# Order of two steps in the vector engine's turn: normalised rows and slots

## The chip, the cores and the metric

The kernel runs on one core of a Trainium2 chip. The metric is the device time of one execution in microseconds (us), the median of several runs. The engines are named as the profile names them: PE (matmul), PEld (its weight load), DVE (vector), ACT (scalar), POOL (GpSimd) and SP (its queue issues most DMAs).

## What is computed

There are 16 graphs of 512 nodes with 128 features. A graph attention layer comes first, then a layer with 16 experts of which each node uses two:

```python
x = x + gnn(layernorm(x), adj, ...)       # 16 graphs, softmax over masked scores, elu
x = x + ffn(layernorm(x), ...)            # top-2 of 16 experts, relu, layernorm with gamma, beta
```

In the second layer the gate's two best experts are found for each node, and the result is the weighted sum of these two experts alone.

## The kernel before

There are two stages. In the graph stage every engine runs a loop of turns over k, written out by hand, and each turn holds steps for several graphs at different depths: in turn k the attention scores are those of graph k, the output of the attention (`elu_parts`, `elu_sum`, L1109 to L1121) and its statistics (`stats`) are those of graph k-2, and the gate and the slots are those of graph k-3. In the expert stage the tokens, sorted by expert in bins in DRAM, are taken in tiles of 128.

Each engine has one in-order queue; what ties them together are semaphores. These steps are near the change:

- `mask(k + 1)` (L1074, DVE): adjacency of the next graph to a bf16 tile `no_edge`.
- `rows(k - 2)` (L1138, DVE): four instructions that make the normalised rows of graph k-2 from `x_sb`, with mean and rstd, into `row_out`. It waits for `s_rs2`, the rstd from POOL, and for the bins' scatters of graph k-6; its end is `s_x2n`.
- `slot(k - 3)` (L1274 to L1308, DVE): 15 small instructions, chained by waits on the engine's own results, that turn the ranks in PSUM `bank[7]` into row numbers of the bins, `slots`. It waits for `s_rank` from PE; its end is `s_slot`.
- POOL in turn k (L581, L567, L572): eight indirect DMAs that scatter the rows of graph k-4 into the bins, the first of which waits for `s_slot` and `s_row_out` of that graph, and between them two rstd computations of two instructions each (`var_eps`, then a pow): the one for the features of graph k+2 after the fourth scatter and the one for the rows of graph k-2 after the fifth (it waits for the `mv` of `stats(k - 2)`).
- PE in turn k: after the first two score blocks, `rows_transposes(k - 3)` (L911) into `bank[7]`, then the logits, later the ranks of the same graph.
- ACT in turn k: `rows_out(k - 3)` copies the rows for the second expert (L709), and `gate_weights(k - 3)` writes their weights.
- SP: the load of the next adjacency waits for `mask`.

The two waits of the PE step are these:

```python
            def rows_transposes(g):
                pe.wait_ge(s_x2n, g + 1)
                wait_for(pe, s_slot, g)
```

Of the kernel before, what the change touches and what calls it, by code (L numbers as in the profile page):

```python
# [19 lines left out]
def graph_attention_and_routed_experts(nc, x, adj, W, a_1, a_2, a_12, W_1, W_2, gate_w, gate_b, w1, b1, w2, b2,  # L20
                                       gamma, beta, out):
    G, N, D = x.shape
# [43 lines left out]
    with ExitStack() as ctx:  # L66
# [162 lines left out]
        def wait_for(eng, s, value):  # L229

            if not isinstance(value, int) or value > 0:
                eng.wait_ge(s, value)
# [39 lines left out]
        def has(k, back):  # L272

            return not isinstance(k, int) or 0 <= k - back < G
# [156 lines left out]
        def bin_wait(eng, g):  # L431

            if g >= 0:
                eng.wait_ge(s_bin[g % RB], 16 * K * TPG * (g // RB + 1))
# [629 lines left out]
        def _(dve):  # L1064
            V = nc.vector
            def xt(k, i):
                t = k * TPG + i
                return x_sb[:, t, :] if isinstance(t, int) else x_sb[:, bass.ds(t, 1), :].rearrange("p a d -> p (a d)")

            def mask(k):  # L1070

                dve.wait_ge(s_adj, 16 * (k + 1))
                wait_for(dve, s_s, k * TPG)
                V.tensor_scalar(no_edge[:, :, :], adj_sb[:, :, :], 0.0, NEG_INF, ALU.is_le, ALU.mult).then_inc(s_mask, 1)  # L1074
# [16 lines left out]
            def scores(k, i):  # L1091

                dve.wait_ge(s_relu, k * TPG + i + 1)
                wait_for(dve, s_pt, (k - 1) * TPG + i + 1)
                settle(dve)
                V.tensor_tensor_reduce(prob[:, i, :], bank[i % 2][:, :], relu4[:, i % 2, :], -ALPHA, 3e38,  # L1096
                                       ALU.add, ALU.min, row_min[:, i:i + 1]).then_inc(s_em, 1)

            def inverse_sums(g):

                dve.wait_ge(s_exp, (g + 1) * TPG)
                V.reciprocal(rinv[:, :], tiles_of(row_sum, g)).then_inc(s_rinv, 1)

            def elu_parts(g, b):

                dve.wait_ge(s_rinv, g + 1)
                dve.wait_ge(s_pv, (g + 1) * TPG)
                for i in range(TPG):
                    last = V.scalar_tensor_tensor(out=z[:, i, :], in0=bank[6][:, i * P:(i + 1) * P],  # L1109
                                                  scalar=rinv[:, i:i + 1], in1=vh[:, b, i, D:2 * D], op0=ALU.mult,  # L1110
                                                  op1=ALU.add)
                last.then_inc(s_z, 1)
            def elu_sum(g):

                zs = Steps(dve, s_zs, g, 2)
                dve.wait_ge(s_z, g + 1)
                zs.did(V.scalar_tensor_tensor(out=xg_of(g), in0=z[:, :, :], scalar=0.0, in1=xg_of(g),
                                              op0=ALU.max, op1=ALU.add))
                dve.wait_ge(s_e, g + 1)
                zs.wait()  # L1120
                zs.did(V.scalar_tensor_tensor(out=xg_of(g), in0=z_exp[:, :, :], scalar=1.0, in1=xg_of(g),  # L1121
                                              op0=ALU.min, op1=ALU.add))
                zs.wait()
                zs.end()

            def feature_shift(g):

                dve.wait_ge(s_rs1, g + 1)
                wait_for(dve, s_feat, g)
                V.scalar_tensor_tensor(out=feat_shift[:, :], in0=mv[:, 0:TPG, 0:1].rearrange("p a b -> p (a b)"), scalar=-1.0,  # L1130
                                       in1=rstd[:, 0:TPG], op0=ALU.mult, op1=ALU.mult).then_inc(s_fshift, 1)

            def rows(g):

                dve.wait_ge(s_rs2, g + 1)
                bin_wait(dve, g - RB)
                for i in range(TPG):
                    last = V.tensor_scalar(row_out[:, g % RB, 0, i, 0:D], xt(g, i), mv[:, TPG + i, 0:1],  # L1138
                                           rstd[:, TPG + i:TPG + i + 1], ALU.subtract, ALU.mult)
                last.then_inc(s_x2n, 1)  # L1140

            def query_weights():

                dve.wait_ge(s_wt_sb, 5)
                dve.wait_ge(s_wt, 3)
                V.tensor_reduce(M_rows[:, 0:1], bank[2][:, 0:D], AX_X, ALU.add).then_inc(s_M, 1)
                dve.wait_ge(s_M, 1)
                V.tensor_scalar(M_rows[:, 1:2], M_rows[:, 0:1], u2[:, 0:1], -1.0 / D, ALU.subtract, ALU.mult).then_inc(s_M, 1)
                dve.wait_ge(s_M, 2)
                V.tensor_scalar(M_sb[:, :], bank[2][:, 0:D], M_rows[:, 1:2], None, ALU.add).then_inc(s_M, 1)  # L1150

            def query_bias():

                dve.wait_ge(s_wt, 4)
                V.scalar_tensor_tensor(out=u1[:, :], in0=bank[1][:, 2 * D:2 * D + 1], scalar=-1.0 / D, in1=u1[:, :],
                                       op0=ALU.mult, op1=ALU.add).then_inc(s_u1, 1)
                V.scalar_tensor_tensor(out=W21[:, :], in0=bank[3][:, 0:2 * D], scalar=-1.0 / D, in1=W21[:, :],
                                       op0=ALU.mult, op1=ALU.add).then_inc(s_W21, 1)
                dve.wait_ge(s_wt, 5)
                dve.wait_ge(s_u1, 1)  # L1160
                V.tensor_tensor(u1[:, :], u1[:, :], bank[0][:, 0:1], ALU.subtract).then_inc(s_u1, 1)

            def first_stats(g):
                dve.wait_ge(s_x[g % 3], 16 * (g // 3 + 1))
                stats(g, 0, s_bn1, s_mv1)

            def bias_cut():

                c = Steps(dve, s_cut, 0, CUTS)
                dve.wait_ge(s_b2, 16)  # L1170
                c.did(V.tensor_copy(b2_part[:, 0, :], b2_rows[:, :]))
                c.wait()
                c.did(V.tensor_tensor(b2_rest[:, 0, :], b2_rows[:, :], b2_part[:, 0, :], ALU.subtract))
                c.wait()
                c.did(V.tensor_copy(b2_part[:, 1, :], b2_rest[:, 0, :]))
                c.wait()
                c.did(V.tensor_tensor(b2_rest[:, 1, :], b2_rest[:, 0, :], b2_part[:, 1, :], ALU.subtract))
                c.wait()
                c.did(V.tensor_copy(b2_part[:, 2, :], b2_rest[:, 1, :]))
                c.end()  # L1180

            def body(k, b, h):
                if k == -2:
                    first_stats(0)
                    query_weights()
                    feature_shift(0)
                    query_bias()
                    return
                if k == -1:
                    mask(0)  # L1190
                    first_stats(1)
                    return
                if k == SPLIT_AT:
                    bias_cut()
                if has(k, 0):
                    scores(k, 0)
                if has(k, 2):
                    elu_parts(k - 2, b)
                if has(k, 0):
                    scores(k, 1)  # L1200
                if k == 0:
                    feature_shift(1)
                if has(k, -2):
                    first_stats(k + 2)
                if k == GROUPS[0][1] + 3:
                    tile_table(0)
                if has(k, 3):
                    gate(k - 3)
                if has(k, 2):
                    elu_sum(k - 2)  # L1210
                    stats(k - 2, TPG, s_bn2, s_mv2)
                if has(k, 1):
                    inverse_sums(k - 1)
                if has(k, 0):
                    scores(k, 2)
                    scores(k, 3)
                if has(k, -2):
                    feature_shift(k + 2)
                if has(k, -1):
                    mask(k + 1)  # L1220
                if has(k, 3):
                    slot(k - 3)
                if has(k, 2) and k < G:
                    rows(k - 2)
                if k == G - 2:
                    dve.wait_ge(s_late, 16 * LATE)
                    dve.wait_ge(s_tab_done, 1)
                    experts.fetch(0)
                if k == G - 1:
                    for t in range(4):  # L1230
                        weights_copy(t)
                    dve.wait_ge(s_b1, 1)
                    V.tensor_copy(b1_cols[:, :], bank[5][:, 0:E * FC]).then_inc(s_b1_cols, 1)
# [301 lines left out]
```

## Time and profile before

| what | value |
| --- | --- |
| time, median of 3 runs | 571.02 us |
| lowest and highest run | 568.17 and 571.75 us |
| span of the profiled execution, first to last instruction | 499.1 us |
| a turn of the graph stage in the middle | 15.27 us |
| busy over the span | PE 85%, PEld 73%, DVE 78%, ACT 64%, POOL 65% |
| granted TensorE clock, mean | 0.953 |

The span leaves out what lies before the first and after the last instruction. Times in the trace count from the span's start. A row of a timeline can hold several equal instructions in a row (x4); its duration then runs from the first start to the last end, and the next instruction can start a little before that end.

### The profile page before, as it was taken

The page shows a single profiled execution, that of the slowest core. Times are in us where ns is not written, and L with a number is a line of the kernel's source. Part 1 is how long each engine was busy: PE and PEld are TensorE (multiplying, and loading weights), DVE is VectorE, ACT ScalarE, POOL GpSimd, SP SyncE. Part 2 cuts the span into 40 slices and gives each one's busy share as a digit, 9 for nine tenths or more (in the row PEclk, how much of TensorE's full clock was granted, in tenths as well). Part 3 has the DMA queues.
Part 4 walks back from the last instruction along what each step waited for, and adds up shares of the span by engine and source line. Part 5 has one row for each costly group of instructions (what it writes and reads, how often), then busy time and mean ns, then how long its engine had stood idle before and what let it go on. Part 6 is the DMA issues. An engine that isn't in the chain of part 4 may idle for free.

```text
span 499.1 us, 11531 instructions
## 1 busy us (share of the span) xinstructions
PE 426.5 (85%) x3175; PEld 364.5 (73%) x3197; DVE 390.3 (78%) x1800; ACT 317.1 (64%) x859; POOL 321.9 (65%) x336
## 2 busy tenths in 40 slices
PE   4869999999998999989989979999999999898000
PEld 3347777776776767767668979999999999798000
DVE  5224788989889898898887968668979997787564
ACT  3468888889877798787774657556665665553000
POOL 2121226776777777866566777788777777777772
PEclk9989999999999999999998999999999999999555
DMA  8632576875366652645611255666777776665522
GB/s 253 196 115 66 195 215 213 262 233 156 73 210 230 178 154 67 224 128 183 178 33 34 65 139 142 170 163 162 198 191 198 199 210 167 153 164 137 129 72 66
DMA packets 82275, 78.84 MB, mean 158 GB/s; under 512 B 7795, under 2 KB 67619, under 8 KB 80934
## 3 DMA queue, kind: packets, MB, share of 16 engines
q1 hardware_dynamic: 73446, 60.99, 42.4%
q0 software_dynamic: 8192, 16.86, 12.6%
q8 instruction: 28, 0.46, 0.4%
q10 hardware_dynamic: 576, 0.26, 0.2%
q14 instruction: 33, 0.27, 0.2%
HBM read 44.44 MB, written 33.65 MB: 156 GB/s over the span
## 4 chain that ended last, share of the span: by engine, by line
PE 47%; DVE 24%; ACT 11%; issue 8%; POOL 5%; DMA 3%; DVEq 1%; ACTq 0%; POOLq 0%; SPq 0%
PE bank L1019 12%; PE bank L1004 11%; POOL yy L634 5%; PE bank L902 4%; PE bank L880 3%; PE bank L862 3%; PE bank L872 3%; DVE no_edge L1074 3%; DVE row_out L1138 3%; DMA yy<-expert_results,slots 3%; PE bank L919 2%; PE bank L991 2%; ACT relu L671 2%; ACT prob L675 2%; PE bank L911 2%
## 5 line engine op out<-in xcount | busy, mean ns | idle before, releaser
L581 POOL DMA_INDIRECT expert_bins<-row_out,slots x128 | 140.2, 1095 | 45.5 <-issue 39.6
L634 POOL DMA_INDIRECT yy<-expert_results,slots x128 | 134.6, 1052 | 39.1 <-issue 33.3
L786 ACT ACTIVATE hidT<-bank,b_cols 128x128 f32<-128x128 f32 x316 | 86.4, 383 | 53.2 <-PE bank L1004 47.5
L1019 PE MATMUL bank<-w_sb,hidT 128*128 x632 | 93.8, 291 | 0.0
L1019 PEld LDWEIGHTS bank<-w_sb,hidT 128*128 128x128 f32 x632 | 84.2, 194 | 2.0
L1004 PE MATMUL bank<-xgT,w_cur 128*128 128x128 f32 x632 | 79.6, 280 | 0.1
L1004 PEld LDWEIGHTS bank<-xgT,w_cur 128*128 128x128 f32 x632 | 75.8, 196 | 0.2 <-issue 0.2
L880 PEld LDWEIGHTS bank<-vh,probT 128*128 128x128 f32 x512 | 63.3, 192 | 14.7 <-issue 13.9
L872 PE MATMUL bank<-featT,qT 128*128 128x512 f32 x128 | 68.2, 615 | 5.2 <-ACT qT L704 2.4
L1096 DVE CUSTOM_DVE_ANT_0 prob<-bank,relu 128x512 f32<-128x512 f32 x64 | 43.5, 682 | 32.9 <-ACT relu L671 29.7
L880 PE MATMUL bank<-vh,probT 128*128 128x128 f32 x512 | 65.5, 276 | 0.5 <-ACT probT L666 0.5
L567 POOL TENSOR_SCALAR var_eps<-mv 128x4 f32<-128x4 f32 x32 | 8.3, 259 | 78.3 <-DVE mv L1085 78.0
L1368 DVE SCALAR_TENSOR_TENSOR y<-bank,xg 128x128 f32<-128x128 f32 x158 | 47.2, 344 | 13.1 <-PE bank L1019 13.0
L675 ACT ACTIVATE prob<-prob,row_min 128x512 f32<-128x512 f32 x64 | 45.8, 716 | 14.6 <-DVE row_min L1096 14.6
L666 ACT COPY probT<-bank 128x512 f32<-128x512 f32 x64 | 37.1, 579 | 25.6 <-PE bank L880 24.7
L671 ACT ACTIVATE relu<-bank 128x512 f32<-128x512 f32 x64 | 37.5, 587 | 7.7 <-PE bank L872 7.7
L794 ACT ACTIVATE final_root<-final_var 128x4 f32<-128x4 f32 x16 | 3.5, 219 | 56.5 <-DVE final_var L1389 56.5
L1337 DVE COPY w_cur<-w_all 128x256 f32 x158 | 36.6, 293 | 3.3 <-issue 1.9
L572 POOL TENSOR_TENSOR rstd<-var_eps,half 128x4 f32<-128x4 f32 x32 | 35.8, 1119 | 5.1 <-ACT feat L716 2.6
L862 PEld LDWEIGHTS bank<-ident,prob 128*128 128x128 f32 x256 | 31.1, 147 | 10.2 <-issue 5.4
L1017 PE MATMUL bank<-b_sum,ones_bf 96*128 x158 | 35.3, 223 | 3.1 <-DVE y L1368 3.1
L862 PE MATMUL bank<-ident,prob 128*128 128x128 f32 x256 | 36.9, 278 | 0.9 <-ACT prob L675 0.9
(143 smaller groups left out, 750.1 us busy)
## 6 DMA issues: line engine op xcount, KB each, us to landing
adj_sb<-in_adj_dram SPq DMA_DIRECT2D x16, 1024.0 KB, 6.4
expert_bins<-xg SPq DMA_DIRECT2D x10, 1032.0 KB, 8.6
expert_results<-y SPq DMA_DIRECT2D x78, 128.0 KB
xg<-expert_bins SPq DMA_DIRECT2D x38, 258.0 KB, 4.1
x_sb<-in_x_dram SPq DMA_DIRECT2D x16, 256.0 KB, 8.5
out_dram<-x_sb SPq DMA_DIRECT2D x15, 256.0 KB
expert_bins<-row_out,slots POOLq DMA_INDIRECT x128, 3.4
w_all<-in_L_ffn_w_dram SPq DMA_DIRECT2D x1, 2048.0 KB, 14.4
```

The lines of the kernel that those rows point to most:

```text
L581: nc.gpsimd.indirect_dma_start(bins[u], bass.IndirectOffsetOnAxis(ap=slots[:, g, i, j:j + 1], axis=0), row_out[:, r, j, i, :], None).then_ ...
L634: nc.gpsimd.indirect_dma_start(yy[:, b, i, j * D:(j + 1) * D], None, results[0:rows, :], bass.IndirectOffsetOnAxis(ap=slots[:, g, i, j:j + 1],
L671: nc.scalar.activation(relu4[:, i % 2, :], bank[i % 2][:, :], ACT.Relu, scale=4.0).then_inc(s_relu, 1)
L675: nc.scalar.activation(prob[:, i, :], prob[:, i, :], ACT.Exp, bias=row_min[:, i:i + 1], scale=-1.0, accum_out=tile_at(row_sum, k, i)).then ...
L786: r = nc.scalar.activation(hidT[:, t % NB, c * P:(c + 1) * P], hidden_of(t, c), ACT.Relu, bias=b1_cols[:, bass.ds(e * FC + c, 1)])
L862: last = nc.tensor.transpose(bank[2 + i % 2][:, c * P:(c + 1) * P], prob[:, i, c * P:(c + 1) * P], ident[:, :])
L872: mm(bank[i % 2][:, :], qT[:, b, i * P:(i + 1) * P], featT[:, b, :], start=False, stop=True).then_inc(s_s, 1)
L880: last = mm(bank[6][:, i * P:(i + 1) * P], probT[:, i % 2, c * P:(c + 1) * P], vh[:, b, c, 0:D], start=(c == 0), stop=(c == TPG - 1))
L1004: m1 = mm(hidden_of(t, c), w1_cur[:, t % WS, c * P:(c + 1) * P], xgT[:, t % NB, :], start=True, stop=True)
L1019: m2 = mm(out_psum(t), hidT[:, t % NB, c * P:(c + 1) * P], w2_sb[:, bass.ds((e * FC + c) * D, D)], start=False, stop=(c == FC - 1))
L1096: V.tensor_tensor_reduce(prob[:, i, :], bank[i % 2][:, :], relu4[:, i % 2, :], -ALPHA, 3e38, ALU.add, ALU.min, row_min[:, i:i + 1]).then_i ...
L1368: V.scalar_tensor_tensor(out=y[:, y_slot(t), :], in0=out_psum(t), scalar=xg[:, v, D:D + 1], in1=xg[:, v, 0:D], op0=ALU.mult, op1=ALU.add). ...
```

## The change

In DVE's turn the rows of graph k-2 are made before the slots of graph k-3; before it was the other way round. Nothing else is changed.

```diff
                 if has(k, -1):
                     mask(k + 1)
+                if has(k, 2) and k < G:
+                    rows(k - 2)
                 if has(k, 3):
                     slot(k - 3)
-                if has(k, 2) and k < G:
-                    rows(k - 2)
                 if k == G - 2:
                     dve.wait_ge(s_late, 16 * LATE)
                     dve.wait_ge(s_tab_done, 1)
```

## Rows read from the trace of the kernel before

**Rows 1.** The page: its span line and the chain's shares by engine.

```profile
span 499.1 us, 11531 instructions
...
PE 47%; DVE 24%; ACT 11%; issue 8%; POOL 5%; DMA 3%; DVEq 1%; ACTq 0%; POOLq 0%; SPq 0%
```

**Rows 2.** Stretches: length; busy us (instructions) by engine; clock; DMA share; GB/s.

```profile
91.98:107.25 15.27, 14.58 (x99) 11.25 (x100) 13.63 (x69) 12.74 (x31) 10.97 (x13) 1.00 0.82 263
```

**Rows 3.** Waits over the whole span: us in total, times, longest us.

```profile
PEld bank L911 <- DVE row_out L1138: 17.0, 14, 1.4
```

**Rows 4.** Timeline of DVE, turn 5: start, us, engine, line, operation, out<-in [idle<-releaser].

```profile
102.46 1.22 DVE L1074 TENSOR_SCALAR no_edge<-adj_sb 128x2048 bf16<-128x2048 int32 x1
103.60 0.17 DVE L1274 SCALAR_TENSOR_TENSOR grown_up<-over,bank 128x16 int32<-128x16 f32 x1
...
105.89 0.29 DVE L1308 TENSOR_REDUCE slots<-picked 128x8 uint32<-128x128 f32 x1
106.09 1.11 DVE L1138 TENSOR_SCALAR row_out<-x_sb,mv,rstd 128x128 f32<-128x128 f32 x4
107.11 0.69 DVE L1096 CUSTOM_DVE_ANT_0 prob<-bank,relu 128x512 f32<-128x512 f32 x1
```

**Rows 5.** Timelines: PE's row transposes behind rows, and behind slots later on.

```profile
107.25 0.66 PE L911 MATMUL bank<-ident,row_out 128*128 128x128 f32 x4 [0.52 <-DVE row_out L1138]
...
289.31 0.29 DVE L1308 TENSOR_REDUCE slots<-picked 128x8 uint32<-128x128 f32 x1
...
289.75 0.63 PE L911 MATMUL bank<-ident,row_out 128*128 128x128 f32 x4 [1.95 <-DVE slots L1308]
```

**Rows 6.** Timeline of POOL: turn 5, and one scatter of a later turn.

```profile
98.14 1.10 POOL L581 DMA_INDIRECT expert_bins<-row_out,slots  x1 [0.20 <-issue]
100.78 0.22 POOL L567 TENSOR_SCALAR var_eps<-mv 128x4 f32<-128x4 f32 x1 [1.54 <-DVE mv L1085]
101.09 1.04 POOL L572 TENSOR_TENSOR rstd<-var_eps,half 128x4 f32<-128x4 f32 x1
102.33 1.48 POOL L581 DMA_INDIRECT expert_bins<-row_out,slots  x1 [0.20 <-issue]
104.11 0.96 POOL L581 DMA_INDIRECT expert_bins<-row_out,slots  x1 [0.30 <-issue]
105.37 0.99 POOL L581 DMA_INDIRECT expert_bins<-row_out,slots  x1 [0.30 <-issue]
107.00 1.03 POOL L581 DMA_INDIRECT expert_bins<-row_out,slots  x1 [0.64 <-issue]
...
199.35 0.98 POOL L581 DMA_INDIRECT expert_bins<-row_out,slots  x1 [0.30 <-DVE slots L1308]
```

**Rows 7.** Timelines of POOL and DVE where the features' pow meets the sums.

```profile
98.33 0.69 DVE L1121 SCALAR_TENSOR_TENSOR x_sb<-z_exp,x_sb 128x512 f32<-128x512 f32 x1
...
205.88 1.60 POOL L572 TENSOR_TENSOR rstd<-var_eps,half 128x4 f32<-128x4 f32 x1
...
206.69 0.69 DVE L1121 SCALAR_TENSOR_TENSOR x_sb<-z_exp,x_sb 128x512 f32<-128x512 f32 x1
...
209.14 0.22 POOL L567 TENSOR_SCALAR var_eps<-mv 128x4 f32<-128x4 f32 x1 [0.36 <-DVE mv L1085]
```

**Rows 8.** Timelines: rows' pow (POOL) and slot's first instruction (DVE), turns 8, 13, 15.

```profile
147.28 1.04 POOL L572 TENSOR_TENSOR rstd<-var_eps,half 128x4 f32<-128x4 f32 x1
...
149.43 0.17 DVE L1274 SCALAR_TENSOR_TENSOR grown_up<-over,bank 128x16 int32<-128x16 f32 x1
...
226.81 1.99 POOL L572 TENSOR_TENSOR rstd<-var_eps,half 128x4 f32<-128x4 f32 x1
...
228.68 0.16 DVE L1274 SCALAR_TENSOR_TENSOR grown_up<-over,bank 128x16 int32<-128x16 f32 x1
...
257.50 1.04 POOL L572 TENSOR_TENSOR rstd<-var_eps,half 128x4 f32<-128x4 f32 x1
...
258.35 0.17 DVE L1274 SCALAR_TENSOR_TENSOR grown_up<-over,bank 128x16 int32<-128x16 f32 x1
```

## The prediction

> **What bounds the kernel now.** First the page's span line and chain by engine [rows 1]: one execution spans 499.1 us, and the chain that ended last is made of PE, DVE and ACT, with DVE 24%. The median of the three runs is 571.02 us, so 71.9 us lie around the span (launch and end), and I carry them over unchanged. The change touches only the turns of the graph stage, so I went from the page to one turn. The table by stretches [rows 2] gives a turn of 15.27 us, in which PE is busy 14.58 us and DVE 13.63 us; POOL is busy 10.97 us, the least of the three. The reader is to see that neither PE nor DVE has more than 1.6 us to spare, and POOL has about four. The waits [rows 3] then show that PE waits at its row transposes (L911) for `row_out` in 14 places: each turn of PE stands still until DVE has finished its pair of slots and rows.
>
> The DVE rows of turn k = 5 [rows 4] give the pair. `mask` starts at 102.46, the first instruction of `slot` at 103.60, the last one (the reduce into `slots`) at 105.89, the four of `rows` at 106.09, and the next turn's `scores` at 107.11. So `slot` takes 106.09 − 103.60 = 2.49 us, `rows` 107.11 − 106.09 = 1.02 us, and the pair 3.51 us, with no gap inside. The last of `rows` ends at 106.09 + 1.11 = 107.20, and the PE transposes start at 107.25 [rows 5]: 0.05 us later.
>
> **The change, part by part.** Nothing is added or removed; 15 instructions of `slot` and 4 of `rows` change places, in 13 turns (k = 3 to 15; in turn 2 there is no `slot`). No DMA moves in any queue. Four things can cost.
>
> 1. What PE waits for. The transposes of graph g wait for `s_x2n` of rows(g) and, in the next line, for `s_slot` of slot(g−1). In turn k DVE makes rows(k−2) and slot(k−3), which are exactly g and g−1 for the transposes of turn k+1. So PE waits for both members of the same pair whichever comes last, and the pair is 3.51 us either way. Rows ready 2.49 us earlier free nobody: cost and gain 0. The last event before the transposes becomes the reduce's end instead of the last row's. From the place of the reduce, 0.20 us before the next instruction with a duration of 0.29 us [rows 4], it will end 0.09 us after `scores` starts; today's last row ends 0.09 us after it too. From its end to PE there is one case: in the expert stage the reduce at 289.31 ended at 289.60 and PE started at 289.75 [rows 5], 0.15 us, where today's rows need 0.05. There PE was coming out of other work, so I take 0 extra per turn, and keep 12 × 0.10 = 1.2 us as the upper bound. From below: the slots ops may lose a few hundredths beside other scatters, or gain them; 12 × 0.05 = 0.6 us of gain is my lower bound, an estimate from the 0.05 us step above.
>
> 2. `rows` needs its rstd from POOL, and now asks for it 2.49 us earlier, at the place where `slot` starts today. That is the new wait, and it stands in front of slot, the next turn's scores and all else on DVE. In turn 5 the pow ends at 101.09 + 1.04 = 102.13 [rows 6], and DVE gets there at 103.60: 1.47 us to spare. I made this subtraction for all 13 turns: eleven have 1.1 to 1.6 us, the tightest of them being turn 8 (147.28 + 1.04 = 148.32 against 149.43) [rows 8]. Two have less than nothing. Turn 13: the pow at 226.81 took 1.99 us, to 228.80, against 228.68. Turn 15 has no mask: 257.50 + 1.04 = 258.54 against 258.35 [rows 8]. With 0.04 us for DVE to start after it, these cost 228.84 − 228.68 = 0.16 and 258.58 − 258.35 = 0.23 us, 0.39 together. PE waits for the pair in both turns, so both go to the end. If that term were hidden it would be 0.
>
> 3. `slots` is ready 1.02 us later, and POOL's first scatter of the next turn waits for it. Today the reduce ends at 105.89 + 0.29 = 106.18 and the scatter starts at 107.00, 0.82 us later [rows 4, 6]. New: the reduce ends at 107.20 and the scatter starts at 108.02. Queued behind it on POOL are three more scatters, the rstd for the features, a fifth scatter, and then the rstd of part 2. Today that last one idles 1.54 us (as in this turn [rows 6], so in the next) until DVE's statistics are there. Against 1.02 us of delay it keeps 0.52 us. But the features' pow shifts into DVE's two-input sums. One turn shows it there: the pow at 205.88 took 1.60 us, to 207.48, just behind the sum that ended at 206.69 + 0.69 = 207.38, and still the next rstd idled 0.36 us and began at 209.14 [rows 7]. In turn 5 the sum's end was 98.33 + 0.69 = 99.02 [rows 7], so the pow would end by about 99.1, the scatter behind it (0.20 us gap, 1.10 us) at 100.4, and var_eps could start at about 100.5, before the 100.78 of today. So the pow of part 2 keeps its place and the term is 0. The cover is thin, 0.3 us. If it is gone, the pow runs into `mask` and ends with it, as in turn 13, and each turn pays the 0.16 us of that turn: 12 × 0.16 = 1.9 us as the bound.
>
> 4. POOL beside `rows`. The moved rows run at 103.60 to 104.7, where POOL finishes one scatter and starts another; today it is `slot` that stands there. The scatter at 102.33 took 1.48 us, to 103.81, against the 0.96 of its neighbours: it ended just behind the mask (102.46 + 1.22 = 103.68) [rows 4, 6]. A scatter that ran beside today's rows, at 199.35, took 0.98 us [rows 6]. Were the held one kept until rows end, it would cost POOL 0.9 us; the two after it would end at about 107.3 instead of 106.36, and the first scatter of the next turn waits until 108.02 anyway. I take 0 for the time. The Trainium skill (SBUF — State Buffer, SBUF: two separate sides) says that VectorE in a two-port mode and GpSimd exclude each other from the shared ports for a whole instruction, which speaks against putting the single-input rows right behind the mask. The mask's row agrees with it, the scatter at 0.98 us does not show it for rows; by the rule the scatter is 0.9 us later, by the row it is not, and the kernel's time is the same by both.
>
> SP's loads wait for none of the moved work: the adjacency load waits for `mask`, which stays in front. ACT's copies for the expert rows come a turn later.
>
> **Sum.** 0 + 0.39 + 0 + 0 = +0.4 us on the profiled span: 499.5, and with the 71.9 around it 571.4 us. Bounds of the same mechanism: 571.0 − 0.6 = 570.4 up to 571.0 + 0.4 + 1.2 + 1.9 = 574.5.
>
> **The rivals.** *POOL closes a loop (slower).* Today nothing leads from POOL's rstd through slots back to POOL, since `slot` comes before `rows`. New there is such a loop: rstd, rows, slot, five scatters, rstd. Its length: 0.04 + 3.51 + 0.09, then 0.82, then from the scatter at 107.00 to the end of the next turn's pow less the idle 1.54. That pow ends one turn behind today's 102.13, at 117.40, which makes 8.86 [rows 2, 4, 6]. Together 13.3 us against a turn of 15.27: 1.9 us in hand. It decides from there. If all five scatters took the 1.48 us of the held one, that is 5 × 0.52 = 2.6 us, 0.7 us too much per turn, 12 × 0.7 = 8 us: 579 us. Against it: only one scatter in a turn is held today. Chance 0.05.
>
> *The soft form:* the pow slips into the mask in most turns, at the 1.9 us of part 3: 573.3 us. For it the thin 0.3 us; against it turn 11, in which the later place was harmless. Chance 0.10.
>
> *PE starts earlier (faster).* If only `row_out` mattered to L911, the idle time in front of it, 0.52 us in a turn [rows 5], would go: 12 × 0.52 = 6.2 us, 564.8 us. Against it stands the second wait in the code, on a slot of the same DVE turn. Chance 0.03.
>
> That the swap does nothing to the order can't be: DVE executes its queue as written.
>
> **How the numbers follow.** Forecast 0.82, soft form 0.10, loop 0.05, PE earlier 0.03. The range takes the forecast's and the soft form's bounds, up to 575, and downwards the scatter of the runs of before, 568.17 to 571.75: 568 to 575. A measurement of this kernel tells about 1%, 5.7 us, from no change. Faster by more than that: 0.03. Slower: the loop and a little for what isn't seen, 0.05. Within: 0.92.
>
> **What would show it.** In the changed profile a middle turn is again 15.2 to 15.4 us. DVE shows `row_out` right behind `no_edge`, then slots, then scores, with no idle time inside except about 0.2 us before `row_out` in turns 13 and 15. PE's wait at L911 names `slots` instead of `row_out`, with the same total of some 17 us. POOL's first scatter starts 0.8 us after the reduce, 1.0 us later than now, and POOL's idle time before var_eps shrinks by about as much. Turns longer than 15.4 us with DVE idle in front of `row_out` would prove the loop; a shorter wait at L911 would prove the PE rival. Wrong in another way would be a change in ACT's or PE's own waits, which this sum holds fixed.

## The result and the profile after

The changed kernel took 576.17 us in the median of 4 runs (574.89 to 585.45), the kernel before 570.66 us beside it (568.17 to 571.75). The ratio is 1.0111, with a 95% interval of 1.0063 to 1.016: slower by 5.5 us between the medians, where 571.4 and no measurable difference had been forecast.

One fact has to stand ahead of everything else. Both kernels run at one of two levels, and all executions of one comparison were at the same one: near 500 us, or, with all its scatter, between 561 and 594 us. The forecast's comparison was at the upper level; the trace of before, with its span of 499.1 us [rows 1], is from the lower one. The changed kernel's own executions show what really lies around a span: its runs of 575.04, 574.89 and 577.31 us had spans of 573.3, 573.1 and 575.5 us. That is 1.7 to 1.8 us, not 71.9. (The ratios leave out disturbed runs, so several of them can't be formed from the medians of all.)

The page of the changed kernel, its span line (the execution of 585.45 us, the longest of the four) and its chain by engine:

```profile
span 583.7 us, 11553 instructions
...
PE 46%; ACT 16%; DVE 15%; issue 12%; another core or an unknown queue 6%; POOL 2%; DMA 1%; DVEq 1%; ACTq 0%; POOLq 0%; SPq 0%
```

Its table by stretches, for a middle turn (columns as in [rows 2], which this row answers), and its waits (us in total, times, longest us), which answer [rows 3]. Their totals are those of the whole span:

```profile
110.68:127.44 16.76, 15.15 (x100) 11.40 (x101) 13.64 (x69) 12.75 (x31) 11.28 (x12) 1.00 0.59 175
```

```profile
POOL expert_bins L581 <- DVE slots L1308: 29.6, 13, 6.8
ACT probT L666 <- PE bank L880: 21.8, 10, 3.3
PEld bank L911 <- issue: 21.1, 15, 4.9
PE bank L911 <- DVE slots L1308: 10.9, 12, 4.5
```

The turn is 16.76 us instead of 15.27, at the same granted clock of 1.00, with the same work in DVE (13.64 against 13.63 us) and PE busy 0.57 us more. DMA moved at 175 GB/s instead of 263, but that says little: the next turn of the trace of before has 187. What became longer is seen in the timeline of DVE, POOL, PE and ACT around L911, which answers [rows 4, 5, 6]:

```profile
105.84 1.22 DVE L1074 TENSOR_SCALAR no_edge<-adj_sb 128x2048 bf16<-128x2048 int32 x1
106.98 1.11 DVE L1138 TENSOR_SCALAR row_out<-x_sb,mv,rstd 128x128 f32<-128x128 f32 x4
108.00 0.16 DVE L1274 SCALAR_TENSOR_TENSOR grown_up<-over,bank 128x16 int32<-128x16 f32 x1
...
110.25 0.29 DVE L1308 TENSOR_REDUCE slots<-picked 128x8 uint32<-128x128 f32 x1
110.45 0.68 DVE L1096 CUSTOM_DVE_ANT_0 prob<-bank,relu 128x512 f32<-128x512 f32 x1
...
110.68 0.63 PE L911 MATMUL bank<-ident,row_out 128*128 128x128 f32 x4 [0.56 <-DVE slots L1308]
...
111.36 0.96 POOL L581 DMA_INDIRECT expert_bins<-row_out,slots  x1 [1.65 <-DVE slots L1308]
...
114.59 1.06 PE L880 MATMUL bank<-vh,probT 128*128 128x128 f32 x8
...
115.14 0.96 POOL L581 DMA_INDIRECT expert_bins<-row_out,slots  x1 [0.30 <-issue]
...
117.21 0.58 ACT L666 COPY probT<-bank 128x512 f32<-128x512 f32 x1 [3.29 <-PE bank L880]
```

The pair on DVE is what the forecast said: rows right behind the mask, then slots, 110.45 − 106.98 = 3.47 us, and PE starts 0.14 us after the reduce's end (110.54). But in the last row ACT's third copy into `probT` of the turn waits 3.29 us for PE. By the trace PE ended the work it waits for at 114.59 + 1.06 = 115.65, and the copy started at 117.21, 1.56 us later. Ends of matmuls are modelled in a trace, so a late end of PE's work can show only at the engine that waits; by the code (`pt_copy`) this copy waits for PE alone, although the profile names `remote` or `issue` for some of them. In front of all copies into `probT` ACT waited 24.7 us for PE in the trace of before; here it is the 21.8 us above and another 21.4 under `remote`. I call the start of this copy, counted from L911 of its turn, **the copy**; here it is 117.21 − 110.68 = 6.53.

### The profile page after: what moved, and what is told of

Same layout as the page of the kernel before. It is cut to its first block, busy times and chain, and to the rows that moved or that the text cites. A ratio compares the mean times of both kernels' runs of the same rounds, so it can differ in the third digit from the quotient of the medians.

```text
span 583.7 us, 11553 instructions
## 1 busy us (share of the span) xinstructions
PE 466.4 (80%) x3197; PEld 388.8 (67%) x3197; DVE 391.9 (67%) x1800; ACT 318.0 (54%) x859; POOL 315.9 (54%) x336
## 3 DMA queue, kind: packets, MB, share of 16 engines
q0 software_dynamic: 8192, 16.86, 10.2%
## 4 chain that ended last, share of the span: by engine, by line
PE 46%; ACT 16%; DVE 15%; issue 12%; another core or an unknown queue 6%; POOL 2%; DMA 1%; DVEq 1%; ACTq 0%; POOLq 0%; SPq 0%
PE bank L1004 13%; PE bank L1019 13%; PE bank L880 3%; PE bank L991 3%; ACT relu L671 3%; ACT prob L675 3%; PE bank L902 2%; PE bank L872 2%; ACT probT L666 2%; POOL yy L634 2%; PE bank L862 2%; DVE no_edge L1074 2%; DVE row_out L1138 2%; PE bank L1017 2%
## 5 line engine op out<-in xcount | busy, mean ns | idle before, releaser
L634 POOL DMA_INDIRECT yy<-expert_results,slots x128 | 132.8, 1038 | 98.6 <-DVE y L1368 45.0
L581 POOL DMA_INDIRECT expert_bins<-row_out,slots x128 | 134.4, 1050 | 69.9 <-issue 38.6
L786 ACT ACTIVATE hidT<-bank,b_cols 128x128 f32<-128x128 f32 x316 | 87.6, 380 | 133.3 <-remote 74.1
L1019 PE MATMUL bank<-w_sb,hidT 128*128 x632 | 105.8, 308 | 10.8 <-issue 10.6
L1004 PE MATMUL bank<-xgT,w_cur 128*128 128x128 f32 x632 | 92.4, 294 | 23.6 <-issue 23.3
L1368 DVE SCALAR_TENSOR_TENSOR y<-bank,xg 128x128 f32<-128x128 f32 x158 | 47.3, 343 | 92.6 <-remote 74.3
L1019 PEld LDWEIGHTS bank<-w_sb,hidT 128*128 128x128 f32 x632 | 93.0, 209 | 17.0 <-issue 14.1
L1004 PEld LDWEIGHTS bank<-xgT,w_cur 128*128 128x128 f32 x632 | 83.4, 206 | 29.3 <-issue 29.2
L880 PEld LDWEIGHTS bank<-vh,probT 128*128 128x128 f32 x512 | 65.2, 195 | 19.5 <-issue 13.9
L880 PE MATMUL bank<-vh,probT 128*128 128x128 f32 x512 | 69.4, 281 | 3.2 <-ACT probT L666 2.7
L666 ACT COPY probT<-bank 128x512 f32<-128x512 f32 x64 | 37.0, 579 | 44.8 <-PE bank L880 21.8
L572 POOL TENSOR_TENSOR rstd<-var_eps,half 128x4 f32<-128x4 f32 x32 | 37.8, 1182 | 5.1 <-ACT feat L716 2.5
L902 PE MATMUL bank<-W,featT 128*128 128x256 f32 x128 | 30.9, 385 | 0.0
```

The costliest lines, as they stand in the source:

```text
L581: nc.gpsimd.indirect_dma_start(bins[u], bass.IndirectOffsetOnAxis(ap=slots[:, g, i, j:j + 1], axis=0), row_out[:, r, j, i, :], None).then_ ...
L634: nc.gpsimd.indirect_dma_start(yy[:, b, i, j * D:(j + 1) * D], None, results[0:rows, :], bass.IndirectOffsetOnAxis(ap=slots[:, g, i, j:j + 1],
L666: nc.scalar.copy(probT[:, i % 2, :], bank[2 + i % 2][:, :]).then_inc(s_pto if i % 2 else s_pte, 1)
L786: r = nc.scalar.activation(hidT[:, t % NB, c * P:(c + 1) * P], hidden_of(t, c), ACT.Relu, bias=b1_cols[:, bass.ds(e * FC + c, 1)])
L880: last = mm(bank[6][:, i * P:(i + 1) * P], probT[:, i % 2, c * P:(c + 1) * P], vh[:, b, c, 0:D], start=(c == 0), stop=(c == TPG - 1))
L1004: m1 = mm(hidden_of(t, c), w1_cur[:, t % WS, c * P:(c + 1) * P], xgT[:, t % NB, :], start=True, stop=True)
```

## The experiments

**Theories.** A: the turn's end is set by ACT's copy, which waits for PE, and at the upper level the place of POOL's scatters against PE's matmuls decides when it starts; the swap moves the first scatter from 0.26 us before L911 (107.00 against 107.25 in [rows 5, 6]) to 0.68 us after it. B: the order on DVE itself costs something (the wait for rstd, rows beside a scatter). C: the changed kernel is merely measured at another moment, and a difference of 1% is the chip's. In the tables below a turn is measured from L911 to L911, for most of the middle turns (5 to 8 and 10 to 12), and the first scatter and the copy are counted from the turn's L911. The expectations, written run by run, use letters of their own and say each time what they mean; their theory S is A here, their R is nearest to B, and the B of p1 is C.

### At the lower level: before, swap, and an earlier release of PE

The two kernels as they are, then each with an earlier release of PE. `s_slots` counts six of the fifteen instructions of `slot`, and PE's wait for the end of the slots of the graph before becomes a wait for the first that is counted, the third instruction, after which the ranks in `bank[7]` have been read:

```diff
             def rows_transposes(g):
                 pe.wait_ge(s_x2n, g + 1)
-                wait_for(pe, s_slot, g)
+                wait_for(pe, s_slots, (g - 1) * SLOT_STEPS + 1 if g else 0)
```

> The kernel before, unchanged, profiled and timed beside itself. Theory A (the swap costs time in the graph stage by a new wait on ACT): a middle turn of the graph stage is 15.3 us as in the first profile of before, the copy of probT behind PE's L880 starts 0.1 us after it, and the time is 571 us within 0.5%. Rival B (the first profile of before came from a quicker state of the chip, and the two profiles differ by that and not by the swap): this profile shows a turn of 16.8 us as that of the changed kernel does, the late copy included, and a span near 569 us.

> The changed kernel, unchanged, beside the kernel before on the same chip. Both theories: slower than before by 0.6 to 1.6% (the first comparison gave 1.0111). Theory A: a middle turn of 16.8 us where before has 15.3; rival B: the turns of both kernels are within 0.3 us of each other and the difference of some 6 us lies elsewhere, most likely in the expert stage.

> The kernel before once more, for its profile on the chip that this call gets. If the chip is the kind on which before takes 570 us: theory A (PE's matmuls are slowed in bursts on that chip, whatever the order of the two steps) expects a graph-stage turn of 16.4 to 16.8 us in which ACT's copy of probT starts about 1.5 us behind PE's modelled end, as in the changed kernel. Theory B (the swap brings these 1.5 us) expects 15.3 us and the copy 0.1 us behind. If before takes 500 us here, both expect 15.28 us.

> The changed kernel. On a chip on which before takes 500 us, both theories expect a ratio of 1.000 to 1.005 and turns of 15.30 us, as in the run before. On one on which before takes 570 us: theory A expects 1.00 to 1.01 with the same turns as before has there, theory B 1.01 with turns 1.4 us longer than before's.

> The changed kernel, in which PE's row transposes wait only until slot has read the ranks out of bank 7 (its first three instructions) and no longer for its end. Theory (the wait for slots of the same DVE turn is what kept the earlier rows from helping): PE's transposes start when scores of PE are done, 0.5 us earlier relative to the pair's end, no wait for DVE at L911; a turn is up to 0.5 us shorter, 14.8 to 15.3 us, and the time 0 to 6 us (0 to 1.2%) less than before. Rival (the turn is closed by another path, through mask, scores and relu, that has no slack of its own): the transposes start earlier but the turn stays at 15.25 to 15.3 us and the time within 0.3%.

> The same release in the order of before: slots first, rows second. All theories: the rows come last, so nothing changes: turns of 15.28 us and a ratio of 1.000 within 0.4%. It is the control that the gain of the other, if any, comes from release and swap together.

| kernel | median us | ratio to before, 95% interval | turn us | first scatter from L911 | copy |
| --- | --- | --- | --- | --- | --- |
| before (p1) | 500.00 | 0.998 (0.9946 to 1.0014) | 15.28 to 15.32 | −0.26 | 5.09 |
| swap (p2) | 502.39 | 1.0029 (0.9988 to 1.007) | 15.29 to 15.35 | +0.67 | 5.06 |
| before (e1) | 499.87 | 1.0005 (0.9964 to 1.0046) | 15.28 to 15.33 | −0.26 | 5.09 |
| swap (e2) | 502.92 | 1.0029 (0.9991 to 1.0066) | 15.30 to 15.36 | +0.67 | 5.06 |
| rows first, early release (e3) | 500.45 | 1.0017 (0.9972 to 1.0062) | 15.05 to 15.10, once 15.27 | +1.46 | 5.53 to 5.59, once 5.76 |
| slots first, early release (e4) | 499.74 | 0.9986 (0.9948 to 1.0023) | 15.27 to 15.32 | −0.26 | 5.09 |

The swap at the lower level (p2): the stretch of a middle turn, and PE, POOL and ACT in it.

```profile
107.42:122.71 15.29, 14.36 (x98) 11.25 (x100) 13.65 (x69) 12.75 (x32) 11.16 (x12) 1.00 0.63 191
```

```profile
107.72 0.63 PE L911 MATMUL bank<-ident,row_out 128*128 128x128 f32 x4 [0.56 <-DVE slots L1308]
...
108.39 0.96 POOL L581 DMA_INDIRECT expert_bins<-row_out,slots  x1 [1.64 <-DVE slots L1308]
...
111.63 1.06 PE L880 MATMUL bank<-vh,probT 128*128 128x128 f32 x8
...
112.78 0.58 ACT L666 COPY probT<-bank 128x512 f32<-128x512 f32 x1 [1.82 <-PE bank L880]
```

The scatter is as late as in the changed kernel (0.67 us after L911), yet the copy comes 112.78 − 112.69 = 0.09 us behind PE's modelled end. From the first L911 (turn 3) to that of turn 15 the two traces of the swap take 186.5 and 186.6 us, and the traces of before 186.12, 186.15 and 186.20: +0.3 to +0.5 us. That this is the forecast's sum of 0.4 is in part luck. Turn 13 contributes 0.08 us of it, the first two turns 0.17 together, and the forecast's 0.23 us of turn 15 lies behind this stretch. Up to turn 17's L911 p2 is 0.7 us longer than p1 (218.45 against 217.72) and e2 2.8 us longer than e1 (219.87 against 217.11); in turn 15 of e2 PE's eight matmuls of L880 took 1.92 us instead of 1.06. Both comparisons give the swap a ratio of 1.0029, some 1.4 us, which can't be told from none. So B, in about the size the forecast gave it, can hold here, and by the intervals the swap costs at most 0.7% at this level.

The early release takes PE's wait for DVE off L911, and the next wait is one block of matmuls later, at the gate's logits, for ACT's copy (e3: PE's row, and the waits in total, times, longest):

```profile
106.61 0.60 PE L911 MATMUL bank<-ident,row_out 128*128 128x128 f32 x4
```

```profile
PEld bank L919 <- ACT x2T L685: 12.9, 14, 2.5
PE bank L919 <- ACT x2T L685: 7.6, 13, 2.1
```

Of the 0.5 us in front of L911 0.2 us per turn is won (15.10 against 15.29), and in the time of the kernel that can't be seen. It needs both edits: with slots first (e4) the turn stays 15.28.

### At the upper level: the two kernels again, and more work on PE

The same two sources met the upper level in the next comparison, on the same chip. Beside them ran the pair with seven matmuls of 128x128 put in front of the block that the copy waits for:

```diff
             def values(g, b, i):
                 if i == 0:
+                    for _ in range(7):
+                        mm(bank[6][:, 0:P], ident[:, :], ones[:, :], start=True, stop=True)
                     wait_for(pe, s_z, g)
```

> The kernel before, for its profile on whatever chip this call gets. On a chip where it takes 500 us: turns of 15.28 us, all theories. On one where it takes 570 us: theory A (PE's results come late in bursts there in either order) turns of 16.4 to 16.8 us; theory B (only the swapped order has them) turns of 15.3 us.

> The changed kernel on the same chip: turns of 15.30 us where before takes 500 us; 16.7 to 16.8 us where before takes 570 us, as in its first profile, by both theories.

> The kernel before with seven idle 128x128 matmuls of PE in front of the first block of values in each turn, so that PE's results come some 1.5 us late at the place where the first profile of the changed kernel showed them late. All theories: turns of 16.7 to 16.9 us and a time 17 to 24 us above before's (12 to 16 turns).

> The changed order with the same seven matmuls. Theory A (a late PE shifts the whole turn and the order of the two steps stays worth nothing): within 1.5 us (0.3%) of the run with slots first, turns longer by 0.02 us. Theory C (once PE is late in the turn, the swapped order costs, for the scatters or the rows' rstd meet other work): 4 to 8 us (0.8 to 1.6%) slower than the run with slots first, with turns 0.3 to 0.6 us longer.

| kernel | median us | ratio to before, 95% interval | turn us | first scatter | PE's modelled end | copy | first L911 to turn 17's |
| --- | --- | --- | --- | --- | --- | --- | --- |
| before (f1) | 575.13 | 1.0185 (0.9917 to 1.0454) | 15.78 to 15.91 | −0.26 | 5.00 | 5.59 to 5.71 | 228.1 |
| swap (f2) | 575.22 | 1.0187 (0.9906 to 1.0468) | 16.75 to 16.83 | +0.68 | 4.97 | 6.52 to 6.60 | 235.7 |
| changed kernel | 576.17 | 1.0111 (1.0063 to 1.016) | 16.71 to 16.79 | +0.68 | 4.97 | 6.48 to 6.56 | 236.1 |
| before, PE late (f3) | 587.37 | 1.0445 (1.0211 to 1.068) | 16.84 to 16.86 | −0.26 | 6.56 | 6.64 to 6.65 | 241.6 |
| swap, PE late (f4) | 589.62 | 1.0421 (1.0251 to 1.0592) | 16.85 to 16.94 | +0.68 | 6.53 | 6.62 to 6.69 | 241.9 |

Before at the upper level (f1), the middle turn and the rows around L911:

```profile
108.72:124.61 15.89, 14.98 (x100) 11.38 (x100) 13.65 (x69) 12.76 (x31) 11.12 (x12) 1.00 0.64 187
```

```profile
108.77 1.03 POOL L581 DMA_INDIRECT expert_bins<-row_out,slots  x1 [0.64 <-issue]
...
109.03 0.66 PE L911 MATMUL bank<-ident,row_out 128*128 128x128 f32 x4 [0.52 <-DVE row_out L1138]
...
112.63 0.96 POOL L581 DMA_INDIRECT expert_bins<-row_out,slots  x1 [0.30 <-DVE mv L1085]
...
112.97 1.06 PE L880 MATMUL bank<-vh,probT 128*128 128x128 f32 x8
...
114.72 0.59 ACT L666 COPY probT<-bank 128x512 f32<-128x512 f32 x1 [2.35 <-PE bank L880]
```

The swap there (f2), the same:

```profile
110.57:127.38 16.81, 15.15 (x100) 11.39 (x100) 13.67 (x69) 12.76 (x32) 11.32 (x12) 1.00 0.58 175
```

```profile
110.87 0.63 PE L911 MATMUL bank<-ident,row_out 128*128 128x128 f32 x4 [0.56 <-DVE slots L1308]
...
111.55 0.96 POOL L581 DMA_INDIRECT expert_bins<-row_out,slots  x1 [1.65 <-DVE slots L1308]
...
114.78 1.06 PE L880 MATMUL bank<-vh,probT 128*128 128x128 f32 x8
...
115.34 0.96 POOL L581 DMA_INDIRECT expert_bins<-row_out,slots  x1 [0.30 <-issue]
...
117.44 0.59 ACT L666 COPY probT<-bank 128x512 f32<-128x512 f32 x1 [3.33 <-remote]
```

Even before is late here: the copy starts at 114.72, 0.69 us behind PE's modelled end of 114.03, and the turn is 15.89 instead of 15.28. In the swap it is 117.44 − 115.84 = 1.60 us late. In both it starts about 1.1 us after the fourth scatter ends: 114.72 − 113.59 = 1.13 and 117.44 − 116.30 = 1.14; in the changed kernel 117.21 − 116.10 = 1.11. The first turn with `rows_transposes`, which has no scatter beside it, is 15.25 us in f1 and 15.34 in f2, as at the lower level. So the swap's later scatters (the first by 0.94 us, the end of the fourth by 0.86) become 0.8 to 1.0 us of later copy and about 0.9 us of longer turn: of the fourteen turns up to turn 17's L911 nine are 0.84 to 1.05 us longer (8.3 us), the other five together 0.7 us shorter, which leaves 7.6 us.

PE itself does not look late. Its next work behind the block, the scores of the same turn, starts 5.02 us after L911 in the swap at the upper level (f2) as at the lower (p2), and so does all that follows up to the next block of L880, 7.74 us after L911 in both:

```profile
115.89 1.02 PE L872 MATMUL bank<-featT,qT 128*128 128x512 f32 x2
...
112.74 1.02 PE L872 MATMUL bank<-featT,qT 128*128 128x512 f32 x2
```

What the traces show to be late is ACT's copy. Whether PE's results, their signal to ACT or ACT itself are held up, they can't tell.

f3 and f4 test this from the other side. With PE's block ending 1.56 us later, at or behind the point that the scatters set, the copy starts 0.08 to 0.15 us behind PE's end, and the order of DVE's two steps is worth only 0.01 to 0.08 us in a middle turn, although the scatters are still 0.94 us apart. The rows of f3 (its lines stand three lower):

```profile
118.29 1.06 PE L883 MATMUL bank<-vh,probT 128*128 128x128 f32 x8
...
119.44 0.59 ACT L666 COPY probT<-bank 128x512 f32<-128x512 f32 x1 [3.31 <-issue]
```

C falls with this: f1 and f2 stand on one chip, moments apart, and their turns differ by 0.9 us with a spread of about 0.1 us within each. In the whole time of the two runs each it is not seen (575.13 and 575.22; before had 571.88 in seven more, from 561.29 to 577.09). How little the totals of this comparison can tell is seen from f1: it is before beside itself, and its ratio is 1.0185. The expert stage gave f2 back 9.6 us against f1 (274.6 us from turn 17's L911 to the end at a granted clock of 0.86, against 284.2 at 0.83), so for a difference in the total only many runs count.

### Only the scatters moved, and no scatters at all

g1 is the kernel before with its order on DVE; only POOL's first scatter of a turn waits for the rows of the same turn as well, and so starts where the swap would have it. g2 and g3 leave out the scatters of both kernels (POOL only raises their semaphore; the experts then see rows that were never written). g4 is the source of e3 again.

```diff
                 if has(k, 4):
                     pool.wait_ge(s_slot, k - 3)
                     pool.wait_ge(s_row_out, k - 3)
+                    wait_for(pool, s_x2n, k - 2 if k - 3 < G else 0)
```

```diff
-                nc.gpsimd.indirect_dma_start(bins[u], bass.IndirectOffsetOnAxis(ap=slots[:, g, i, j:j + 1], axis=0),
-                                             row_out[:, r, j, i, :], None).then_inc(s_bin[r], 16)
+                pool.sem_inc(s_bin[r], 16)
```

> The order of before (slots, then rows), and POOL's first scatter of a turn waits for the end of rows too, so that it starts some 0.8 us after PE's row transposes as with the swap, and not 0.25 us before them. If this call again gets the slow mode, in which before takes 570 us: theory S (the later scatters are what makes PE's results later with the swap) expects turns of 16.6 to 16.8 us; rival R (the release of PE by slots and not by rows, or the work that DVE does then) expects turns of 15.9 us as before has in that mode. In the mode in which before takes 500 us both expect 15.3 us.

> The swapped order without the scatters of the rows into the bins (their semaphores are raised, the DMAs are left out, so the experts see blank rows). In the slow mode: theory S expects turns of 15.3 to 15.9 us, rival R 16.8 us. In the mode of 500 us: 15.2 to 15.3 us.

> The order of before without the scatters. In the slow mode: theory S expects turns equal to those of the swap without scatters within 0.1 us and below 15.9 us; rival R expects 15.9 us, 0.9 us less than the swap without them. In the mode of 500 us: 15.2 to 15.3 us.

> Rows first with the early release of PE's row transposes, which had turns of 15.10 us in the mode of 500 us. In the slow mode: if what is late there is PE's own rate, 16.4 to 16.8 us, and if the lateness hangs on the release by the end of slots, 15.9 us or less.

| kernel, one execution each | time us | turn us | first scatter | copy |
| --- | --- | --- | --- | --- |
| before, beside them | 569.41 | | | |
| before, scatters late (g1) | 583.09 | 16.79 to 16.93 | +0.83 | 6.61 to 6.75 |
| swap, no scatters (g2) | 543.68 | 15.28 to 15.30 | none | 5.05 to 5.06 |
| before, no scatters (g3) | 543.69 | 15.22 to 15.23 | none | 5.09 |
| rows first, early release (g4) | 573.84 | 16.67 to 16.72, once 16.96 | +1.40 | 7.16 to 7.21, once 7.45 |

Before with late scatters (g1; its lines stand one lower) and the two without scatters (g2, then g3):

```profile
107.91 0.66 PE L912 MATMUL bank<-ident,row_out 128*128 128x128 f32 x4 [0.52 <-DVE row_out L1139]
...
108.74 0.96 POOL L581 DMA_INDIRECT expert_bins<-row_out,slots  x1 [1.73 <-DVE row_out L1139]
...
112.53 0.96 POOL L581 DMA_INDIRECT expert_bins<-row_out,slots  x1 [0.30 <-issue]
...
114.54 0.58 ACT L667 COPY probT<-bank 128x512 f32<-128x512 f32 x1 [3.29 <-remote]
```

```profile
105.14:120.43 15.29, 14.62 (x100) 11.25 (x100) 13.59 (x69) 12.75 (x32) 2.53 (x4) 1.00 0.51 174
```

```profile
106.97:122.19 15.22, 14.65 (x100) 11.24 (x101) 13.59 (x69) 12.76 (x31) 2.53 (x4) 1.00 0.50 170
```

With DVE's old order and late scatters the turn is that of the swap (16.83 against 16.81), and the copy stands 114.54 − 113.49 = 1.05 us behind the fourth scatter. Without scatters the lateness is gone from these turns in both orders, at the same level of the chip, since the whole is 543.7 us and not 500. The two orders then differ by 0.06 us a turn. That is theory A, by both sides: in the graph stage it is the scatters' start that costs, not the order on DVE. (Each kernel ran once here, but each trace has seven such turns.) g4 shows the early release of little use here: its scatters start 1.40 us after L911, the copy follows 1.0 us behind the fourth (114.27 − 113.27), and 0.1 of the 0.2 us is left.

### Trying to win it back: POOL's order

If the copy is late only beside the scatters, POOL's queue can be ordered so that they run elsewhere. In h2 and h3 the rstd of the features comes before the four scatters, and the fifth scatter after the rows' rstd; h1 is the swap beside them.

```diff
                     settle(pool)
+                    if has(k, -2):
+                        rstds(0, k + 3, s_mv1, s_rs1)
                     scatter_row(k - 4, 0, 0)
...
-                if has(k, -2):
+                elif has(k, -2):
                     rstds(0, k + 3, s_mv1, s_rs1)
-                if has(k, 4):
-                    scatter_row(k - 4, 2, 0)
                 if has(k, 2) and k <= G:
                     rstds(TPG, k - 1, s_mv2, s_rs2)
                 if has(k, 4):
+                    scatter_row(k - 4, 2, 0)
```

> The changed kernel in more rounds. In the slow mode (before at 570 us) the graph stage of the changed kernel ended 7.6 us later in its trace: if the rest of the kernel passes it on, the ratio is 1.008 to 1.016, if the expert stage gives part of it back, 1.003 to 1.008. In the mode of 500 us: 1.000 to 1.005.

> The order of before on DVE; on POOL the features' rstd comes ahead of the four scatters instead of behind them, and the fifth scatter behind the rows' rstd. The scatters then run from about 5 us after PE's row transposes instead of from the same moment. Theory S (PE's results are late only while scatters run): in the slow mode PE's first block of values is not late and the turn falls from 15.9 to 15.3 to 15.6 us, the time by 3 to 7 us; or the lateness turns up at a later block. If the place of the scatters did not matter: 15.9 us as before. In the mode of 500 us: 15.3 us.

> The same move on POOL with the swapped order on DVE. POOL's first scatter no longer waits for slots, so the swap should not move the scatters: turns within 0.1 us of the run with slots first, in either mode. If the swap itself made PE late in the slow mode, 0.9 us more.

| kernel | median us | ratio to before, 95% interval | turn us | copy | first L911 to turn 17's |
| --- | --- | --- | --- | --- | --- |
| swap (h1) | 586.96 | 1.0148 (1.0095 to 1.0201) | 16.79 to 16.89 | 6.55 to 6.64 | 236.8 |
| before, POOL moved (h2) | 579.14 | 0.9957 (0.9897 to 1.0017) | 15.24 to 16.64 | 5.08 to 5.21 | 229.1 |
| swap, POOL moved (h3) | 586.92 | 1.0141 (1.0053 to 1.0228) | 16.05 to 16.77 | 5.05 to 5.06 | 238.0 |

The runs of before on this chip spread from 576.37 to 593.78 us (median 586.05 of all 17), so the totals tell little: by the medians the swap is 0.9 us above before and h2 6.9 us below it, by the ratios 1.5% above and 0.4% below. The copy is on time again in h2 and h3, as A has it, but most turns are not short again. In h2's long turns the lateness can stand further down, beside the scatters that were moved there. The next copy of turn 8 (its lines stand one lower) comes 11.76 us after L911 behind a wait for PE, where in p1 it comes at 9.48 without one:

```profile
148.24 1.84 POOL L581 DMA_INDIRECT expert_bins<-row_out,slots  x1 [0.30 <-issue]
...
149.89 0.59 ACT L667 COPY probT<-bank 128x512 f32<-128x512 f32 x1 [2.05 <-PE bank L881]
```

Against the expectation h3 is not within 0.1 us of h2: its middle turns are 16.05 to 16.77 us. Why the order on DVE still matters there was not settled. No order of POOL's steps that I ran beat the kernel before by an amount that can be told.

## Why the prediction was wrong

**The carry-over of 71.9 us failed first.** The sum was made on a span of 499.1 us, and all that the timed runs had above it was called launch and end. Measured, it is 1.7 us; the other 70 were in the execution itself, at the upper level. Of the 77.0 us between the spans of e1 and f1, before at both levels on one chip, 63.2 stand behind turn 17's L911 and 11.0 between turn 3's and turn 17's:

```profile
276.20:497.20 221.00, 176.34 (x1564) 172.27 (x1564) 172.38 (x750) 107.37 (x367) 164.18 (x154) 0.91 0.59 153
...
290.00:574.20 284.20, 208.26 (x1564) 193.37 (x1564) 172.69 (x750) 108.89 (x366) 161.47 (x154) 0.83 0.45 119
```

The price for the change was thus worked out on a trace whose kernel did not run at the level on which it was timed.

**Part 3 (slots and the first scatter) is the step that failed in the sum.** Its times were right: the scatter starts at 111.36, 0.82 us after the reduce ends at 110.54, and 0.68 us behind L911, where it had been 0.25 before it. The term was 0, with 1.9 us as a bound, because only what is queued behind the scatter on POOL was costed; ACT's wait for PE was taken as fixed. At the lower level that holds in the middle turns (most 15.29 to 15.30 us against 15.28). At the upper one the copy for which ACT waits on PE starts about 1.1 us after the fourth scatter and moves with it, and the term measured 0.84 to 1.05 us in each of nine turns and 7.6 us up to turn 17, more than the 5.5 us between the medians. g1, which moved the scatters alone, shows this term by itself; g2 and g3 show it gone with the scatters.

**Part 1 (what PE waits for) was right.** The wait at L911 changed its name to slots and PE starts 0.14 us after the reduce, close to the 0.15 us taken from [rows 5]. The pair takes 3.47 us. Turn by turn the middle turns of p2 are 0 to 0.03 us longer than those of p1, below the bound of 0.10.

**Part 2 (rows' wait for rstd) was right**, and its size too: in turn 13 the mask starts at 240.48 and rows at 241.78 in the changed kernel, 1.30 us where a turn without the wait has 1.14 (105.84 to 106.98), so 0.16 us, the number of the forecast. In turn 15 rows start at 276.91, 0.23 us behind the start of DVE's instruction before them (276.68), where `slot` had started together with it in p1 (259.72): again the forecast's number.

**Part 4 (POOL beside rows) was right.** In the changed kernel the scatter at 105.59 took 1.59 us, to 107.18, 0.12 us behind the mask's end of 107.06; before, the held one ended 0.13 us behind it [rows 4, 6]. Rows run from 106.98 to 108.09, and the next scatter, at 107.49, took 0.96 us beside them. So the mask holds a scatter and the rows don't. Of the Trainium skill's rule (SBUF — State Buffer, SBUF: two separate sides), that VectorE in a two-port mode and GpSimd shut each other out for a whole instruction, the mask's row bears out the one half, and no run here shows it for the rows.

**The rivals.** The loop on POOL did not close: the longest wait of DVE in front of `row_out` that the profiles of f2 and of the changed kernel show is 0.15 us, in turn 15. PE did not start earlier, since the second wait in the code binds; e3 shows that without it 0.2 us a turn could be had at the lower level, not 0.52, since ACT's copy is the next wait. What happened was none of the rivals. It is nearest to the last sentence of the forecast, a change in ACT's waits, which the sum had held fixed.

**What stays open.** What puts the chip at the upper level, and by what path POOL's scatters delay ACT's copy, was not settled. The traces of the upper level show it as a fact of the graph stage's middle turns: the delay ends about 1.1 us after the fourth scatter, the granted clock of the turn reads 1.00 throughout, and where no scatter runs there is no delay. That the 5.5 us between the medians are these turns is argued and not shown: the expert stage of single runs varies by more than that, and of the three comparisons at the upper level that have the swap, the first (1.0111) and the last (1.0148) have intervals clear of 1, but in the last the medians are only 0.9 us apart, and the second can't tell.

## What to carry to other kernels

Set the span of the profiled execution against the timed runs before anything is added to it: a remainder of 70 us on 500 is no launch cost but a sign that the trace shows the kernel in a different condition from the one in which it is timed, and then a term of 0 is only a 0 of that condition. When a step is moved, follow each semaphore to the DMAs that it starts and ask what other engines do at that moment, not only what is queued behind them. And an end that is modelled, as a matmul's is, can't show that its result was late: read the wait of the engine that takes it, and beside it the starts of the next matmuls.

## What the runs showed that was not expected

- Two levels of the same source on the same chips: before at 499.87 us in one comparison and 575.13 in the next on one chip, with the mean clock at 0.959 and 0.912. In the graph stage the granted clock is 1.00 in the middle turns of both.
- Most of what lies between the levels is in the expert stage (221.0 against 284.2 us), at a granted clock of 0.91 against 0.83. ACT's hidden layer (L786), which by the code waits for PE, has 89.5 us of waits there in f1 that the profile names `remote`, and DVE's `y` (L1368) 61.9; in e1 neither has any. g3, without scatters, still has 41.1 and 57.3, so the scatters do not account for this part.
- ACT's copy started 0.69 us (before) and 1.60 us (swap) behind PE's modelled end at the upper level, 0.09 us at the lower.
- Taking away all scatters saved 26 us of 569.41, to 543.7, of which some 11.5 us stand between the L911 of turns 3 and 17 (216.7 us in g3; 228.1 in f1, on another chip). The experts of g3 work on rows that were never written, so the rest says little.
- A scatter starts 0.82 us after the DVE instruction that releases it has ended, in [rows 4, 6] and in the changed kernel alike.
